# A ViT block in one kernel: other jobs between the last column sums and the output products, turns among the output products, and GpSimd's clearing ahead of its table loads

## Chip, cores, metric

One core of a Trainium2 chip (trn2). The metric is the device time of one execution in microseconds (us); lower is better.

## The reference

Sixty-four images of 224 x 224 x 3 go through patch embedding, one attention layer and a mixture-of-experts feed-forward layer, in float32:

```
h = tok(x)                                # 16x16 patches, layernorm, 768->192, layernorm, cls token, + position
h = concat([cls_tok, h], axis=1)          # (64, 198, 192)
qkv = (layernorm(h) @ qkv_w.T)            # 12 heads of 64
attn = (q @ k.T + q . (tab_kv[iv] + tab_kh[ih])) * scale    # relative positions by row (iv) and column (ih)
attn = softmax(attn)
out = attn @ v + attn . (tab_vv[iv] + tab_vh[ih])
h = h + out.reshape(b, n, 768) @ proj_w.T + proj_b
h = h + shared_mlp(n) + top2_of_8_experts(n)    # n = layernorm(h), hidden relu squared
```

## The kernel before

Three stages follow each other, each with its own buffers and one hand-written program per engine; what one stage computes for the next lies in device memory. `tokens_stage` makes the tokens, `attention_stage` the attention layer, `experts_stage` the rest.

**Tokens stage.** Eight groups of eight images (GROUPS, GB), 14 patch columns (SIDE) each. At a group's end VectorE scales the 14 tiles of normalised rows (L303) and signals `rows_normed`; GpSimd multiplies them by a gain (L221) and adds the positions (L224), and SP's queue stores them. In the last group the work is split: VectorE signals after the first POOLED = 6 tiles, which GpSimd finishes, and finishes the other 8 itself (L311, L315). SP stores the two parts with two DMAs (L156), GpSimd's part first.

**Attention stage, the step.** A group has 16 token tiles and six head pairs (PAIRS); a pair takes 16 steps (8 images x 2 heads), a group 96 steps. Step i of every engine is the same list of pieces. TensorE: scores of step i (L1077), transposes of the probabilities of step i-2 (L1043), the weighted sum of step i-3 (L1060), then the jobs that the table gives to this step. VectorE: the row maximum (L870), the reciprocal of the sums of step i-1 (L862), two copies of the weighted sum of step i-3 (L854, L855), then its part of the jobs. ScalarE: a copy of the transposed probabilities (L712), the exponentials (L724), then its part of the jobs. GpSimd multiplies the probabilities by the reciprocal (L631). Each waits by semaphore for the piece that it reads; the engines run in order, so whoever is behind with a job is behind with the next step.

**Attention stage, the jobs.** `spread` (three times: first, middle and last group) writes the order of the jobs of each pair and spreads them over its 16 steps by COST, a number for each kind. All jobs use four PSUM banks (RING = 4) in turn, in this order, so a job also waits until the job four places ahead of it has been read out. For pair p the jobs are, with the letters of the code:

- f(Q), f(K), f(R), f(C): queries and keys of the next pair (L998), then their products with the row tables (L1002) and column tables (L1008); ScalarE copies the first three kinds, VectorE adds C (L814).
- v: values for two pairs (L1016), copied by ScalarE (L703).
- l(0..3), l(4..7): for the pair just finished, the value-side sums by rows (L1020, added by VectorE at L822) and by columns (L1026, added at L831). l(7) is a short one.
- l(8..15): the output products (L1031), added to the residual by VectorE (L841). l(8) reads all of the column sums, so it waits for l(7)'s addition.
- t(0..7), once per group, for the next group: a turn (L991, L992) transposes two normalised tiles. ScalarE copies the high parts (L681, L682), VectorE writes the low parts (L799, L800) and normalises the two tiles of the turn after next (L780). A query block Q[j] reads turns 2j and 2j+1.

**Attention stage, the opening.** Before the first step the weights are transposed (`prep`, L952 and L953) with the first group's eight turns among them, and the first pair's jobs are done without steps. GpSimd makes the one-hot rows, issues the table DMAs (L612, L613), clears `kx`, `qx` and `rx` (L615, L616, L618), and copies the one-hot rows into `kx` (L624). VectorE spreads the tables (L910, L923) when they have landed; TensorE waits for that, for the copies and for the clearing, and then does `opening[TURN:]`, whose first eight jobs are Q and K.

## Time and profile before

| | |
|---|---|
| median of 3 runs | 4431.72 us (4425.48 to 4433.78) |
| the profiled execution | 4426.74 us, its span 4425.0 us |
| mean granted TensorE clock | 0.963 |
| TensorE busy | 4084.1 us (92%) |
| VectorE busy | 2922.1 us (66%) |
| ScalarE busy | 2506.7 us (57%) |
| GpSimd busy | 1273.7 us (29%) |

The tokens stage lasts until 418 us, the attention stage's opening until 509.6, its steps until about 3488, the experts stage until the end. A busy time counts an instruction from its start to its end, waiting inside it included. The granted clock is a share of 2.4 GHz; it has two levels, 1.00 and 0.50. The page also has an idle time before each group of instructions and what ended it.

### The profile page before, as it was taken

The numbers are of one execution on the slowest core, as the hardware profiler recorded it, in microseconds if no ns is written. First come the engines' busy times: TensorE is split into PE (matmuls) and PEld (weight loads), VectorE is DVE, ScalarE is ACT, GpSimd is POOL, SyncE is SP. The second block draws the span as 40 slices with busy tenths as digits, with TensorE's granted clock in tenths as the row PEclk, the third lists the DMA queues.
The fourth block names the chain that finished last, engine by engine and source line by source line (L and its number), as shares of the span: only waits on it lengthen the run. The fifth ranks groups of instructions, "written<-read, shape, count | busy, mean of one in ns | idle before, by whom it ended". The sixth has DMA issues, their size and how long they took to land. (4 is left out here: it accounts for less than half of the span.)

```text
span 4425.0 us, 84814 instructions
## 1 busy us (share of the span) xinstructions
PE 4084.1 (92%) x28203; PEld 3987.8 (90%) x28203; DVE 2922.1 (66%) x7468; ACT 2506.7 (57%) x6685; POOL 1273.7 (29%) x1423
## 2 busy tenths in 40 slices
PE   4986799899999999989989999999999799999999
PEld 4885699899899999989989998998999699999999
DVE  4675666666666766666666666666666577777776
ACT  2553666566666666656666666666665344444443
POOL 1232322222232222213222222221322244444443
PEclk8997899999999999999999999999999799999999
DMA  8543000000000000000000000000000222222222
GB/s 184 131 109 73 7 1 1 1 24 1 1 23 1 1 2 23 1 1 23 1 1 19 7 1 2 23 1 1 12 1 1 66 90 89 89 89 89 89 89 87
DMA packets 88973, 161.67 MB, mean 37 GB/s; under 512 B 5705, under 2 KB 75936, under 8 KB 85054
## 3 DMA queue, kind: packets, MB, share of 16 engines
q1 hardware_dynamic: 85118, 152.66, 12.1%
q0 software_dynamic: 944, 2.42, 0.3%
q8 instruction: 182, 2.98, 0.3%
q10 hardware_dynamic: 2576, 2.36, 0.2%
q14 instruction: 153, 1.25, 0.1%
HBM read 127.82 MB, written 29.60 MB: 36 GB/s over the span
## 5 line engine op out<-in xcount | busy, mean ns | idle before, releaser
L631 POOL TENSOR_TENSOR att_prob<-att_prob,att_total 99x396 f32<-99x396 f32 x768 | 650.9, 848 | 2279.0 <-DVE att_total L862 2279.0
L712 ACT ACTIVATE att_probT<-att_t 99x396 f32<-99x396 f32 x768 | 385.0, 501 | 737.4 <-PE att_t L1043 732.0
L870 DVE TENSOR_REDUCE att_npeak<-att_s 99x2 f32<-99x396 f32 x768 | 435.4, 567 | 451.7 <-PE att_s L1077 437.2
L724 ACT ACTIVATE att_prob<-att_s,att_npeak 99x198 f32<-99x198 f32 x1536 | 638.0, 425 | 80.3 <-DVE att_npeak L870 77.5
L1077 PE MATMUL att_s<-att_kx,att_qx 96*99 96x198 f32 (+1 forms) x3072 | 661.9, 339 | 4.5 <-DVE att_xres L841 2.3
L1060 PE MATMUL att_o<-att_probT,att_vx 99*96 99x198 f32 (+1 forms) x3072 | 663.1, 339 | 1.1 <-DVE att_rx L855 1.1
L1257 POOL TENSOR_TENSOR ffn_hidden<-ffn_relu 128x384 f32<-128x384 f32 x462 | 419.7, 914 | 494.8 <-ACT ffn_relu L1286 492.7
L1077 PEld LDWEIGHTS att_s<-att_kx,att_qx 96*99 96x99 f32 (+1 forms) x3072 | 494.3, 170 | 16.3 <-issue 5.3
L1286 ACT ACTIVATE ffn_relu<-ffn_h 128x384 f32<-128x384 f32 x462 | 226.3, 490 | 477.3 <-PE ffn_h L1503 476.5
L1515 PE MATMUL ffn_y<-ffn_down,ffn_hidden 128*128 128x192 f32 x2772 | 487.5, 326 | 0.0
L1060 PEld LDWEIGHTS att_o<-att_probT,att_vx 99*96 99x96 f32 (+1 forms) x3072 | 477.2, 181 | 5.8 <-issue 1.4
L1515 PEld LDWEIGHTS ffn_y<-ffn_down,ffn_hidden 128*128 128x128 f32 x2772 | 457.8, 190 | 1.2 <-issue 0.2
L854 DVE COPY att_oT<-att_o 64x198 f32<-64x198 f32 x768 | 277.1, 361 | 240.7 <-PE att_o L1060 233.2
L1043 PEld LDWEIGHTS att_t<-att_ident,att_prob 99*99 99x99 f32 x3072 | 396.1, 170 | 37.5 <-issue 21.9
L1043 PE MATMUL att_t<-att_ident,att_prob 99*99 99x99 f32 x3072 | 405.0, 255 | 20.3 <-ACT att_probT L712 16.5
L855 DVE COPY att_rx<-att_o 32x198 f32<-32x198 f32 x768 | 404.1, 526 | 10.4
L1408 DVE TENSOR_TENSOR ffn_hidden<-ffn_hidden,ffn_gates 64x384 f32<-64x384 f32 (+1 forms) x528 | 362.4, 702 | 20.5 <-issue 3.8
L1031 PE MATMUL att_p<-att_pw,att_oT 128*99 128x192 f32 x1536 | 292.6, 334 | 80.9 <-DVE att_oT L831 80.9
L1031 PEld LDWEIGHTS att_p<-att_pw,att_oT 128*99 128x99 f32 x1536 | 247.7, 169 | 89.6 <-issue 88.1
L724 ACT ACTIVATION_READ_ACCUMULATOR att_prob<-att_s,att_npeak 99x1 f32 x1536 | 313.3, 204 | 0.0
L814 DVE TENSOR_TENSOR att_qx<-att_p,att_qx 32x448 f32<-32x448 f32 (+1 forms) x384 | 226.4, 590 | 63.7 <-PE att_p L1008 35.4
L348 PE MATMUL tok_y<-tok_w,tok_patchT 128*112 128x192 f32 x1344 | 249.6, 339 | 10.5 <-DVE tok_y L282 10.5
(237 smaller groups left out, 8170.7 us busy)
## 6 DMA issues: line engine op xcount, KB each, us to landing
ffn_gates<-gate_rows SPq DMA_DIRECT2D x66, 768.0 KB, 5.0
tok_pixels<-in_x SPq DMA_DIRECT2D x24, 1568.0 KB
ffn_hid<-hidden SPq DMA_DIRECT2D x35, 288.0 KB, 3.0
att_xres<-hidden SPq DMA_DIRECT2D x8, 1188.0 KB
hidden<-att_xres SPq DMA_DIRECT2D x8, 1188.0 KB
ffn_acc<-hidden SPq DMA_DIRECT2D x33, 288.0 KB, 2.9
out_hidden<-ffn_acc SPq DMA_DIRECT2D x33, 288.0 KB, 2.4
hidden<-tok_rows SPq DMA_DIRECT2D x7, 1176.0 KB
```

Source lines behind the costliest of these rows:

```text
L631: nc.gpsimd.tensor_tensor(prob[:, i % 2, :, :], prob[:, i % 2, :, :], view(total[:, i % 2, :], [[1, 2], [0, NTOK]]), ALU.mult).then_inc(pr ...
L712: nc.scalar.activation(probT[:, i % 2, :], t_bank[0:HALF, 0:2 * NTOK], ACT.Copy).then_inc(probT_made, 1)
L724: ins = nc.scalar.activation(prob[:, i % 2, h, :], s_bank[i % 2][0:HALF, h * NTOK:(h + 1) * NTOK], ACT.Exp, bias=npeak[:, i % 2, h:h + 1], ...
L855: nc.vector.tensor_copy(view(rx[ext:ext + 32, p % 2, :], [[GB, NTOK]], b), o_bank[ext:ext + 32, 0:NTOK]).then_inc(outs_used, 1)
L870: nc.vector.tensor_reduce(npeak[:, i % 2, :], s_bank[i % 2][0:HALF, 0:2 * NTOK].rearrange("p (h k) -> p h k", h=2), AX.X, ALU.max, negate= ...
L1031: ins = nc.tensor.matmul(bank[0:HALF, t * DIM:(t + 1) * DIM], oT[:, s, cols], pw[:, weights, :], start=True, stop=True)
L1043: ins = nc.tensor.transpose(t_bank[0:HALF, k * NTOK + h * HALF:k * NTOK + (h + 1) * HALF], prob[:, j % 2, h, k * HALF:(k + 1) * HALF], ide ...
L1060: ins = nc.tensor.matmul(o_bank[0:M, 0:NTOK], vx[:, 2 * b + k, p % 2, v0:v0 + M], probT[:, j % 2, k * NTOK:(k + 1) * NTOK], start=(k == 0) ...
L1077: ins = nc.tensor.matmul(s_bank[i % 2][0:HALF, h * NTOK:(h + 1) * NTOK], qx[0:K, p % 2, head, q0:q0 + HALF], kx[0:K, p % 2, head, b * NTOK ...
L1257: nc.gpsimd.tensor_tensor(hidden[0:rows, s, j, :], relu[0:rows, (n + 2 * s) % 4, :], relu[0:rows, (n + 2 * s) % 4, :], ALU.mult).then_inc( ...
L1408: ins = nc.vector.tensor_tensor(hidden[lo:hi, s, j, :], hidden[lo:hi, s, j, :], gates[lo:hi, s, e, :], ALU.mult)
L1515: ins = nc.tensor.matmul(y_bank[t][:, 0:DIM], hidden[:, s, j, t * 128:(t + 1) * 128], down[:, j, :], start=(n == 0), stop=(n == HT - 1))
```

## The change

1. In the jobs of every pair, l(5) and l(7) go up; l(6, 7), a key or value job and f(C[2], C[3]) stand together ahead of l(8). Before, l(7, 8) were neighbours.
2. Four turns, t(0) to t(3), stand among the output products of the fifth pair of a group (`turning`), one behind each second one. Before, two. The sixth pair (`ending`) begins with the other four.
3. In the opening GpSimd clears `kx` and `qx` right after the one-hot rows, copies into `kx`, clears `rx`, and only then issues the table DMAs. TensorE does the eight Q and K jobs before it waits for tables and buffers.
4. In the last group of the tokens stage POOLED is 5, and GpSimd starts when all 14 tiles are scaled.

```diff
-    POOLED = 6
+    POOLED = 5
...
-                        if wv == (SIDE if more else POOLED) - 1:
-                            ins.then_inc(rows_normed, 1)
+                    ins.then_inc(rows_normed, 1)
                     if not more:
-                        ins.then_inc(last_normed, 1)
-                        dve.wait_ge(last_normed, 1)
+                        dve.wait_ge(rows_normed, GROUPS + PRIMED)
...
                 if ending and not last:
-                    jobs = f(Q[0]) + t(2) + f(K[0]) + t(3) + f(Q[1]) + t(4) + f(K[1]) + t(5) + f(Q[2]) + t(6) + f(K[2])
-                    jobs += t(7) + f(Q[3], K[3]) + l(0) + f(R[0])
+                    jobs = f(Q[0]) + t(4) + f(K[0]) + t(5) + f(Q[1]) + t(6) + f(K[1]) + t(7) + f(Q[2], K[2], Q[3], K[3])
+                    jobs += l(0) + f(R[0])
...
-                jobs += l(4) + f(C[0]) + k(2) + l(5) + f(C[1]) + l(6) + k(3) + f(C[2]) + l(7, 8) + f(C[3])
-                jobs += l(9, 10, 11, 12) + (t(0) if turning else []) + l(13, 14) + (t(1) if turning else []) + l(15)
+                jobs += l(4) + f(C[0]) + l(5) + k(2) + f(C[1]) + l(6, 7) + k(3) + f(C[2], C[3])
+                for j in range(8, 16):
+                    jobs += l(j) + (t((j - 9) // 2) if turning and j % 2 else [])
...
+                nc.gpsimd.memset(kx[:], 0.0).then_inc(keys_cleared, 1)
+                nc.gpsimd.memset(qx[:], 0.0).then_inc(keys_cleared, 1)
+                pool.wait_ge(onehot_made, 9)
+                pool.wait_ge(keys_cleared, 2)
+                for s in range(2):
...
+                pool.wait_ge(keys_made, 4)
+                pool.wait_ge(prep_full, PAIRS)
+                nc.gpsimd.memset(rx[:], 0.0).then_inc(zeroed, 1)
                 for half in range(2):
                     for i, tab in enumerate((tab_kv, tab_kh)):
...
                 spread_onehot()
+                for j in opening[TURN:TURN + 8]:
+                    job(0, -1, "opening", *j)
                 pe.wait_ge(tables_made, 1)
                 pe.wait_ge(keys_made, 4)
                 pe.wait_ge(zeroed, 1)
                 pe.wait_ge(tables_in, 16 * 16)
-                for j in opening[TURN:]:
+                for j in opening[TURN + 8:]:
                     job(0, -1, "opening", *j)
```

TensorE's order in the third pair of the first group, from the third column sum on (L1026 value-side columns, L998 a key block, L1008 query-side columns, L1031 output products; L1077, L1043 and L1060 are the fixed products of a step). Before, the last rows of it:

```order
628 L998 MATMUL att_p<-att_x0h,att_w0h 128x396
...
632 L998 MATMUL att_p<-att_x,att_w1l 128x396
633 L1008 MATMUL att_p<-att_q,att_tq 72x112 x4
634 L1077 MATMUL att_s<-att_kx,att_qx 99x198 x2
635 L1043 MATMUL att_t<-att_ident,att_prob 99x99 x4
636 L1060 MATMUL att_o<-att_probT,att_vx 128x198 x2
637 L1026 MATMUL att_p<-att_rx,att_tv 128x112 x2
638 L1031 MATMUL att_p<-att_pw,att_oT 99x192 x2
```

And now:

```order
627 L1026 MATMUL att_p<-att_rx,att_tv 128x112 x2
628 L998 MATMUL att_p<-att_x0h,att_w0h 128x396
...
632 L998 MATMUL att_p<-att_x,att_w1l 128x396
633 L1077 MATMUL att_s<-att_kx,att_qx 99x198 x2
634 L1043 MATMUL att_t<-att_ident,att_prob 99x99 x4
635 L1060 MATMUL att_o<-att_probT,att_vx 128x198 x2
636 L1008 MATMUL att_p<-att_q,att_tq 72x112 x6
637 L1031 MATMUL att_p<-att_pw,att_oT 99x192 x2
```

The short column product (L1026 x2) has moved ahead of the key block, a step's fixed products and both pieces of query columns (x6); before, the output product was the next row.

TensorE's order at the end of the fifth pair of that group (L991 belongs to a turn, four rows each). Before:

```order
956 L1031 MATMUL att_p<-att_pw,att_oT 99x192 x4
957 L1077 MATMUL att_s<-att_kx,att_qx 99x198 x2
958 L1043 MATMUL att_t<-att_ident,att_prob 99x99 x4
959 L1060 MATMUL att_o<-att_probT,att_vx 96x198 x2
960 L991 MATMUL att_p<-att_ident,att_norm 128x99
...
964 L1031 MATMUL att_p<-att_pw,att_oT 99x192 x2
965 L1077 MATMUL att_s<-att_kx,att_qx 99x198 x2
```

And now:

```order
957 L1031 MATMUL att_p<-att_pw,att_oT 99x192 x2
958 L991 MATMUL att_p<-att_ident,att_norm 128x99
...
962 L1031 MATMUL att_p<-att_pw,att_oT 99x192 x2
963 L1077 MATMUL att_s<-att_kx,att_qx 99x198 x2
964 L1043 MATMUL att_t<-att_ident,att_prob 99x99 x4
965 L1060 MATMUL att_o<-att_probT,att_vx 96x198 x2
966 L1031 MATMUL att_p<-att_pw,att_oT 99x192 x2
967 L991 MATMUL att_p<-att_ident,att_norm 128x99
```

There is a turn in each of the last four steps, where there were turns in two.

GpSimd's order in the opening now (before, the five DMAs stood ahead of the clearing, and the copies last):

```order
48 L608 MEMSET att_kx 128x6336
49 L609 MEMSET att_qx 128x6336
50 L615 COPY att_kx<-att_onehot 32x1584 x4
51 L619 MEMSET att_rx 96x3168
52 L623 DMA att_tabT<-in_L_attn_tab_kv 64x30x1
53 L623 DMA att_tabT<-in_L_attn_tab_kh 64x30x1
54 L623 DMA att_tabT<-in_L_attn_tab_kv 64x30x1
55 L623 DMA att_tabT<-in_L_attn_tab_kh 64x30x1
56 L624 DMA att_pbias<-in_L_attn_proj_b 99x192
```

The clearing has moved up by five DMAs, and the DMAs stand last.

## Rows read from the trace of the kernel before

**Rows 1.** Windows, the steps of the attention stage: length; busy times; clock, DMA share, GB/s.

```profile
core 0: us, PE busy (x) PEld busy (x) DVE busy (x) ACT busy (x) POOL busy (x), PEclk, DMA share, GB/s
509.60:3488.00 2978.40, 2811.90 (x20399) 2752.26 (x20397) 1926.04 (x4671) 1871.08 (x5475) 721.62 (x896) 0.98 0.02 7
```

**Rows 2.** Waits of TensorE, same stretch: us in total, times, longest.

```profile
PE att_p L1031 <- DVE att_oT L831: 80.9, 48, 2.3
PE att_p L998 <- DVE att_x L800: 31.1, 7, 4.4
PE att_p L998 <- issue: 20.2, 14, 2.1
```

**Rows 3.** Timelines of VectorE and TensorE, third pair of the fourth group: start, length.

```profile
1779.42 0.45 DVE L831 TENSOR_TENSOR att_oT<-att_p,att_oT 128x224 f32<-128x224 f32 x1
...
1780.12 0.86 PE L1031 MATMUL att_p<-att_pw,att_oT 128*99 128x192 f32 x4 [1.75 <-DVE att_oT L831]
1780.82 0.83 PE L1077 MATMUL att_s<-att_kx,att_qx 128*99 128x198 f32 x4
...
1782.52 0.55 PE L1008 MATMUL att_p<-att_q,att_tq 128*72 128x112 f32 x4
```

**Rows 4.** Timeline of TensorE, sixth pair of that group.

```profile
1922.82 0.67 PE L998 MATMUL att_p<-att_x0h,att_w0h 128*128 128x396 f32 x1 [4.45 <-DVE att_x L800]
```

**Rows 5.** Windows behind three waits of that group.

```profile
1720.00:1724.00 4.00, 4.00 (x18) 3.58 (x18) 1.20 (x3) 1.22 (x5) 0.85 (x1) 0.57 0.02 4
...
1922.00:1928.00 6.00, 5.18 (x18) 4.91 (x19) 2.02 (x6) 2.88 (x8) 0.85 (x1) 0.50 0.00 0
...
1942.00:1946.00 4.00, 4.00 (x16) 3.82 (x15) 1.07 (x4) 3.60 (x9) 0.85 (x1) 0.57 0.00 0
```

**Rows 6.** Timeline of GpSimd in the opening.

```profile
433.70 1.05 POOL L612 DMA_DIRECT2D att_tabT<-in_L_attn_tab_kv  x1 [9.08 <-issue]
...
436.37 5.40 POOL L615 MEMSET att_kx<- 128x6336 f32 x1
...
449.83 6.18 POOL L624 COPY att_kx<-att_onehot 32x1584 f32<-32x1584 f32 x4
```

**Rows 7.** Timelines of VectorE and TensorE in the opening.

```profile
441.95 7.93 DVE L780 TENSOR_SCALAR att_norm<-att_xres,att_mv,att_sd 99x192 f32<-99x192 f32 x1
...
451.50 0.43 PE L991 MATMUL att_p<-att_ident,att_norm 99*128 99x99 f32 x1 [17.94 <-DVE att_norm L780]
...
454.49 0.35 DVE L799 TENSOR_TENSOR att_x0l<-att_p,att_x0h 128x198 fp32r<-128x198 f32 x1
...
480.85 0.70 PE L998 MATMUL att_p<-att_x0h,att_w0h 128*128 128x396 f32 x1 [2.70 <-DVE att_vx L923]
```

**Rows 8.** The tables' tile: time from issue to landing of its DMAs.

```profile
DMA to landing us min/median/max: 7.4/8.6/9.8
```

**Rows 9.** Timelines of the tokens stage's end; last, the line that waits for the store.

```profile
400.60 8.83 DVE L303 TENSOR_SCALAR tok_rows<-tok_y,tok_mv,tok_rstd 112x192 f32<-112x192 f32 x14
...
402.51 2.68 POOL L221 TENSOR_TENSOR tok_rows<-tok_rows,tok_g 112x1152 f32<-112x1152 f32 x1 [27.79 <-DVE tok_rows L303]
...
411.26 1.76 DVE L315 TENSOR_TENSOR tok_rows<-tok_rows,tok_posb 112x1536 f32<-112x1536 f32 x1
...
L158 SPq EVENT_SEMAPHORE  x1: 17/17/17, 418.2 to 418.2; - x1
```

**Rows 10.** Timelines of GpSimd and VectorE in the experts stage.

```profile
3602.27 0.83 POOL L1257 TENSOR_TENSOR ffn_hidden<-ffn_relu 128x384 f32<-128x384 f32 x1 [2.00 <-ACT ffn_relu L1286]
3602.45 1.05 DVE L1408 TENSOR_TENSOR ffn_hidden<-ffn_hidden,ffn_gates 64x384 f32<-64x384 f32 x1
...
3603.52 0.56 DVE L1408 TENSOR_TENSOR ffn_hidden<-ffn_hidden,ffn_gates 64x384 f32<-64x384 f32 x1
```

**Rows 11.** Windows of a fifth pair's end and the sixth's start; VectorE's timeline at a turn.

```profile
1899.00:1915.00 16.00, 16.00 (x111) 15.56 (x112) 13.41 (x35) 7.09 (x25) 3.39 (x4) 1.00 0.01 2
1915.00:1938.00 23.00, 16.72 (x99) 15.82 (x98) 12.16 (x35) 14.88 (x43) 3.39 (x4) 0.85 0.00 1
...
1907.22 0.36 DVE L799 TENSOR_TENSOR att_x0l<-att_p,att_x0h 128x198 fp32r<-128x198 f32 x1 [0.28 <-ACT att_x L682]
...
1907.99 0.67 DVE L780 TENSOR_SCALAR att_norm<-att_xres,att_mv,att_sd 99x192 f32<-99x192 f32 x2
```

More of the change, by code:

```diff
@@ L114, in tokens_stage @@
         channel_in = [m.sem(f"channel_in{c}") for c in range(CH)]
-        last_normed, last_scaled, last_made = m.sem("last_normed"), m.sem("last_scaled"), m.sem("last_made")
+        last_scaled, last_made = m.sem("last_scaled"), m.sem("last_made")
         consts_in, weights_in, ident_made = m.sem("consts_in"), m.sem("weights_in"), m.sem("ident_made")
@@ L607, in _ @@
                 nc.gpsimd.tensor_tensor(onehot[:, :], onehot[:, :], rowhot, ALU.add).then_inc(onehot_made, 1)
+                nc.gpsimd.memset(kx[:], 0.0).then_inc(keys_cleared, 1)
[3 more added lines that the diff above has]
+                for s in range(2):
+                    for lo, head in ((64, 0), (32, 1)):
+                        pool.wait_ge(keys_made, 2 * s + head)
+                        nc.gpsimd.tensor_copy(view(kx[lo:lo + 32, s, head, :], [[NTOK, GB], [1, NTOK]]),
+                                              view(onehot[:, :], [[0, GB], [1, NTOK]])).then_inc(keys_made, 1)
+                pool.wait_ge(keys_made, 4)
+                pool.wait_ge(prep_full, PAIRS)
+                nc.gpsimd.memset(rx[:], 0.0).then_inc(zeroed, 1)
                 for half in range(2):
@@ L614, in _ @@
                                ).then_inc(consts_in, 16)
-                nc.gpsimd.memset(kx[:], 0.0).then_inc(keys_cleared, 1)
-                nc.gpsimd.memset(qx[:], 0.0)
-                pool.wait_ge(prep_full, PAIRS)
-                nc.gpsimd.memset(rx[:], 0.0).then_inc(zeroed, 1)
-                pool.wait_ge(zeroed, 1)
-                pool.wait_ge(keys_cleared, 1)
-                for s in range(2):
-                    for lo, head in ((64, 0), (32, 1)):
-                        pool.wait_ge(keys_made, 2 * s + head)
-                        nc.gpsimd.tensor_copy(view(kx[lo:lo + 32, s, head, :], [[NTOK, GB], [1, NTOK]]),
-                                              view(onehot[:, :], [[0, GB], [1, NTOK]])).then_inc(keys_made, 1)
                 pool.wait_ge(consts_in, 16 * 5)
```

## The prediction

> **What bounds the kernel now.** The page's shares (in the table above) say that TensorE is the busiest engine by far, so time can only go where TensorE stands still or runs at its lower clock. The windows say how much of that the attention stage holds [rows 1]: 2978.4 us with TensorE busy 2811.9, so 166 us idle, and a mean granted clock of 0.98. The waits of TensorE in that stage name the idle time [rows 2]: 80.9 us in 48 waits of an output product (L1031) for a sum of VectorE (L831), 31.1 us in 7 waits of a query product (L998) for a turned tile (L800), and 20.2 us in 14 more at L998, which the profile calls "issue". The timelines then show each kind once.
>
> First kind [rows 3]: VectorE does the short last sum at 1779.42 to 1779.87, and the first output product, which reads it, starts at 1780.12 after 1.75 us of idle time. In the order it is the job right behind the product that this sum is made of.
>
> Second kind [rows 4]: a query product starts at 1922.82 after 4.45 us. It needs turn 3, and turn 3 is the job right ahead of it in the order; ScalarE's copies of a query and a key block stand in that queue ahead of the turn's. Turns 5 and 7 have the same neighbours, which are the 14 waits of 1.4 us.
>
> The clock [rows 5]: it is granted at 0.57 in the 4 us that begin with the end of such an L1031 wait, which is 1.7 us lost; two of these in this group of images make 3.4 us. Behind the 4.45 us wait it is 0.50 for 6 us (1.2 GHz, 3.0 us lost), and at 1942 it falls again (0.57, 1.7 us): with the 0.3 us until it is back, 5.0 us per group.
>
> **The opening, in steps.** GpSimd has two table DMAs issued by 424.6, then 9.08 us pass, and its clearing only begins at 436.37; the copies of the one-hot rows end it [rows 6]. VectorE's first normalise starts at 441.95 and takes 7.93 us where two of them take 0.67 elsewhere [rows 7, 11]: it ends when the third clearing ends, at 449.8. The next three end with one GpSimd copy each, so the first low part starts at 454.49. In the change the two large clearings stand at 422.5 to 433.3, the four copies to 439.5, the third clearing to 442.2. The normalises then meet 0.2 us of it. TensorE's first turn (451.50 now) comes at about 442.7, and the low part 1.6 us behind it, when ScalarE has copied, at 444.3. From there VectorE is busy without a gap, so all of it shifts: **-10.2 us** (bounds -13 and -5: clearing gone wholly, or DMA issues in the way as a copy is now, about 1.5 us for each normalise).
>
> The table DMAs move behind that: issued from 442.2, with the same 14 us of issuing, and 7.4 to 9.8 us to land [rows 8], they are there at about 465. VectorE wants them when preparation ends, 477.5 - 10.2 = 467.3. If they were 7 us late nobody on the path would mind, for the eight query and key products now go ahead of the wait for tables. TensorE's first stands at 480.85 behind 2.70 us of idle time, released by the last table copy [rows 7]: **-2.7** (bounds -3.2, -1). ScalarE takes 11 us for these eight, and that covers the tables; its own wait, for the key buffers, is met far earlier.
>
> **The last group of the tokens stage.** Now the 14 scalings take 8.83 us, since two of them stand behind GpSimd's operations of 2.68 us, then VectorE's own two take 1.76 each and end at 413.02 [rows 9]. In the change all 14 run undisturbed (0.29 us apart, ending at 404.7), but then two-input operations of both engines start together: VectorE with 9 tiles (1.98 us each), GpSimd with 5 (2.2 each). Such a pair stands in the experts stage [rows 10]: VectorE's product, started 0.18 us behind GpSimd's, takes 1.05 us against 0.56, so it waits for it. In turns they end at 404.8 + 8.3 = 413.1, GpSimd probably last; and SP's queue issues the 5-tile store first, so both stores start there. The last landing is now 5.2 us behind VectorE's end [rows 9], with 8 tiles on the way; with 14 it is between 0 and 3.9 us more (6 x 5.2 / 8), and I take **+2.5 us**. Unhindered, both would end at 409.3 and it would be -1.5. The Trainium skill ("SBUF — State Buffer", Who interferes with whom) has a rule against this edit: a VectorE operation with two SBUF inputs and a GpSimd operation that reads SBUF exclude each other for their whole length. The trace agrees (1.05 against 0.56 us), so the sum goes by +2.5 and not by -1.5.
>
> **Between last column sums and output products.** The short product now goes up; behind it come a key or value product, the fixed products of a step (1.7 us, from 1780.82 to 1782.52 [rows 3]), and the last two pieces of query columns, then the first output product: about 3.8 us of TensorE work, in which VectorE has some 2 us of its own ahead of the sum. Of 80.9 us, 2.0 stay (the last pair of the last group and the closing have nothing to put between), 16.1 (7 x 2.3, the longest, in the pair with turns) belong to the next term, and of the remaining 62.8 I keep 3: **-60 us** (bounds -63, -45). What is late next is the pile on VectorE behind it: both pieces of query columns and a residual sum in one step, by my count 4.2 us against TensorE's 3.5. The probabilities of two steps on are then ready 0.2 us before they are wanted; the -45 is for that cover gone.
>
> **Turns among output products.** Four turns instead of two fall in the last steps of the fifth pair. There VectorE is already busy 13.41 of 16 us while TensorE is 16.00 of 16 [rows 11]. Each turn costs it 1.35 us (two low parts and two normalises, 1907.22 to 1908.57), two more make 16.1, and it waits up to half a microsecond for ScalarE at each. So VectorE becomes the limit. In the sixth pair there are then four turns instead of six, the first two queries need turns long done, and the last two have another product between. Following the new order by hand with these durations I get six waits of 0.4 to 1.6 us, 5.6 in all per group, against (16.1 + 31.1 + 20.2) / 7 = 9.6 now: 7 x 4.0 = **-28 us** (bounds 0 and -67).
>
> **Clock.** The 3.4 us per group around plain waits is 27 us in 8 groups; with the waits goes most of it, **-24** (bounds -27, 0). Of 5.0 us in each of 7 groups I expect 2.1 to stay, since waits of 1.6 us can bring it: **-20** (bounds -35, 0).
>
> **Sum:** -10.2 - 2.7 + 2.5 - 60 - 28 - 24 - 20 = -142.4. The profiled execution took 4426.7 us; the median of the three runs, 4431.7, is 0.1% above. 4426.7 - 142.4 = 4284. The experts stage is not touched.
>
> **Rivals.** *The turn stretch stays as it is* (4332 us): VectorE's pile brings as much waiting as before, and the clock falls as often; -94.4 only. For it speaks 13.41 of 16; against it that no single wait can be as long as the 4.45. *Nothing is left* (4224 us): all 67 us and all 62 us of clock come back and the opening gives its 13: +2.5 - 13 - 63 - 67 - 62 = -202.5. *The waits move* (4400 us): L1031's wait turns into one of the transposes (L1043) for GpSimd's product, whose slack is 0.2 us by my count; the opening's 10.4 and some 15 us stay. *Slower* (4526 us): between the middle of the fifth pair and that of the sixth the many short waits hold TensorE at 1.2 GHz throughout. The stretch holds 16.0 + 16.7 = 32.7 us of its work [rows 11], which costs 7 x (32.7 - 5.0) = +194 against -94.4. It decides from the point where the clock is low for 57% of that work (7 x 32.7 x 0.57 - 35 = 95). Against it: over 23 us with 6.3 us idle, the 4.45 us in one piece, the mean clock was still 0.85 [rows 11]. The Trainium skill ("TensorE: Matmul & The Clock Gate", A second HAM failure mode: psum-queue depth-cycling) describes this mechanism: frequent short idle times between groups of products make the gate swing between its levels. The trace has single falls, no such series.
>
> **Chances.** Forecast 0.58 (4255 to 4315), turn stretch unchanged 0.20, nothing left 0.08, waits move 0.09, slower 0.05. The range 4235 to 4345 takes the first two and a little of the third. 0.2%, 9 us, is about what a measurement of this kernel can tell from no change: faster 0.93, same 0.02, slower 0.05.
>
> **What would show it.** L780's longest falls from 7.93 to under 3 us; the first L998 comes 10 to 13 us earlier (some 470); L1031 waits for L831 only once or twice; L998 has no 4 us wait; the stage's clock is 0.99; waits of 0.4 to 1.6 us appear at L1043 and L1060 around the fifth and sixth pair. I am wrong if L1043's waits exceed 60 us, or if the clock stays at 0.98.

## The result and the profile after

The changed kernel takes 4251.28 us (median of 4 runs, 4251.08 to 4252.45), the kernel before 4432.75 us (4 runs, 4425.48 to 4436.11): ratio 0.9595, 95% interval 0.9581 to 0.961. The forecast was 4284 us in a range of 4235 to 4345, so the measured time lies in the range, 33 us below the forecast and 27 us above the nearest rival (4224). The gain is 181 us where 142 were forecast.

Its page, with the lines that stand in the table of before:

```profile
span 4249.3 us, 84755 instructions
PE 4023.5 (95%) x28203; PEld 3931.1 (93%) x28203; DVE 2890.2 (68%) x7468; ACT 2501.6 (59%) x6685; POOL 1274.0 (30%) x1423
PEclk8998799999999999999999999999999899999999
```

The span divides at two events: the first score product (L1077) and the first transpose of the experts stage (L1472).

| us | before | after | difference |
|---|---|---|---|
| up to the first scores | 509.8 | 496.0 | -13.7 |
| steps of the attention stage | 2987.1 | 2825.1 | -162.0 |
| experts stage | 928.1 | 928.1 | 0 |

**The steps.** Windows over them in both kernels (length, TensorE busy, clock), of after:

```profile
core 0: us, PE busy (x) PEld busy (x) DVE busy (x) ACT busy (x) POOL busy (x), PEclk, DMA share, GB/s
495.90:3306.20 2810.30, 2752.98 (x20399) 2695.74 (x20397) 1905.62 (x4670) 1866.53 (x5475) 720.47 (x896) 1.00 0.02 7
```

Of before, the same stretch was 2972.20 us with 2811.80 busy. So TensorE stood idle for 160.4 us and now for 57.3: 103.1 us less. The other 58.8 us are the same 20,399 products done faster, which is the clock. Read in windows of 2 us, with (1 - granted clock) added up, the steps lost 71.7 us in 34 falls of the clock, and now lose 10.3 us in 2, one at 540 and one at the very end of the stage. The turn stretch of the fourth group, of which [rows 11] have the windows, stands some 85 us earlier now (both kernels are in the last steps of the fifth pair in the first window, and in the first of the sixth in the second):

```profile
1814.00:1830.00 16.00, 14.32 (x102) 13.31 (x100) 14.48 (x39) 7.14 (x26) 3.04 (x4) 1.00 0.01 2
1830.00:1853.00 23.00, 20.46 (x136) 18.95 (x135) 17.36 (x48) 18.75 (x59) 5.42 (x7) 1.00 0.00 1
```

VectorE is busy 14.48 of 16 us, more than TensorE's 14.32: it is the fuller engine there, as the prediction feared. But the 23 us behind it hold 20.46 us of TensorE at full clock, where they held 16.72 at 0.85.

The waits of TensorE in the steps (us in total, times, longest), against [rows 2]:

```profile
PE att_t L1043 <- POOL att_prob L631: 29.7, 37, 1.3
PE att_t L1043 <- ACT att_probT L712: 16.2, 18, 1.3
PE att_p L1031 <- DVE att_oT L831: 2.0, 2, 1.2
```

L1031's 48 waits (80.9 us) are 2 (2.0 us), and both kinds at L998 (51.3 us) are gone. New are the waits at L1043 for GpSimd's scaled tile, 3.9 us before. 78.9 + 51.3 - 25.8 = 104.4 is close to the 103.1 of the windows. The wait for ScalarE was 16.5 us before and is not the change's.

The new waits stand where turns lie among output products. VectorE's and GpSimd's rows ahead of such a wait in the third group, and TensorE's rows with a wait there (start, length):

```profile
1470.76 1.02 DVE L841 TENSOR_TENSOR att_xres<-att_p,att_xres 99x384 f32<-99x384 f32 x2
1471.69 0.56 DVE L870 TENSOR_REDUCE att_npeak<-att_s 99x2 f32<-99x396 f32 x1
1472.16 0.16 DVE L862 RECIPROCAL att_total<-att_total 99x2 f32<-99x2 f32 x1
1472.40 0.85 POOL L631 TENSOR_TENSOR att_prob<-att_prob,att_total 99x396 f32<-99x396 f32 x1 [3.43 <-DVE att_total L862]
```

```profile
1473.30 0.59 PE L1043 MATMUL att_t<-att_ident,att_prob 99*99 99x99 f32 x4 [1.30 <-POOL att_prob L631]
1477.11 0.59 PE L1043 MATMUL att_t<-att_ident,att_prob 99*99 99x99 f32 x4 [0.20 <-POOL att_prob L631]
1480.98 0.59 PE L1043 MATMUL att_t<-att_ident,att_prob 99*99 99x99 f32 x4 [0.94 <-POOL att_prob L631]
1489.40 0.59 PE L1043 MATMUL att_t<-att_ident,att_prob 99*99 99x99 f32 x4 [1.33 <-POOL att_prob L631]
```

GpSimd is free, but gets its reciprocal late, since VectorE has a turn's writes, two residual sums (L841) and a maximum ahead of it: the pile that the prediction saw, five waits and 4 us a group. No fall of the clock stands behind any of these waits.

**The opening.** The four first normalises in one row, before:

```profile
441.95 12.62 DVE L780 TENSOR_SCALAR att_norm<-att_xres,att_mv,att_sd 99x192 f32<-99x192 f32 x4
```

VectorE's and GpSimd's timelines of after, against [rows 6, 7]:

```profile
432.62 4.26 DVE L758 BATCH_NORM_STATS2 att_stat<-att_xres 99x6 f32<-99x192 f32 x16 [7.96 <-DMA att_xres<-hidden]
439.98 3.29 DVE L780 TENSOR_SCALAR att_norm<-att_xres,att_mv,att_sd 99x192 f32<-99x192 f32 x4
443.82 0.36 DVE L799 TENSOR_TENSOR att_x0l<-att_p,att_x0h 128x198 fp32r<-128x198 f32 x1 [0.56 <-ACT att_x L682]
```

```profile
422.04 5.37 POOL L608 MEMSET att_kx<- 128x6336 f32 x1
427.36 5.37 POOL L609 MEMSET att_qx<- 128x6336 f32 x1
432.86 6.17 POOL L615 COPY att_kx<-att_onehot 32x1584 f32<-32x1584 f32 x4
439.10 2.73 POOL L619 MEMSET att_rx<- 96x3168 f32 x1
447.05 1.05 POOL L623 DMA_DIRECT2D att_tabT<-in_L_attn_tab_kv x1 [3.08 <-issue]
```

The four normalises took 12.6 us in all, each ending at about the end of a GpSimd operation; now they take 3.29. The first low part comes at 443.82 rather than 454.49. The gap before the third table transfer is 3.08 us where it was 9.08 [rows 6], and the tables' tile lands faster than in [rows 8]:

```profile
DMA to landing us min/median/max: 3.6/3.8/4.2
```

TensorE's first query product, against the 480.85 of [rows 7], comes at once behind the last work before it:

```profile
466.72 0.51 PE L965 MATMUL att_s<-att_ident,att_onehot 32*99 32x32 f32 x2 [4.17 <-DVE att_w1l L773]
467.15 0.70 PE L998 MATMUL att_p<-att_x0h,att_w0h 128*128 128x396 f32 x1
```

**The last group of tokens**, VectorE and GpSimd, against [rows 9]:

```profile
399.00 4.15 DVE L303 TENSOR_SCALAR tok_rows<-tok_y,tok_mv,tok_rstd 112x192 f32<-112x192 f32 x14
403.18 1.96 DVE L309 TENSOR_TENSOR tok_rows<-tok_rows,tok_g 112x1728 f32<-112x1728 f32 x1
405.18 3.84 DVE L313 TENSOR_TENSOR tok_rows<-tok_rows,tok_posb 112x1728 f32<-112x1728 f32 x1
...
403.23 3.98 POOL L221 TENSOR_TENSOR tok_rows<-tok_rows,tok_g 112x960 f32<-112x960 f32 x1 [30.04 <-DVE tok_rows L303]
407.28 3.80 POOL L224 TENSOR_TENSOR tok_rows<-tok_rows,tok_posb 112x960 f32<-112x960 f32 x1
```

They end in turns, some 2 us apart: VectorE's at 405.14, GpSimd's at 407.21, VectorE's at 409.02, GpSimd's at 411.08.

The tokens stage ahead of L298 scatters by up to 4 us from one profile to another, so the opening is compared in two pieces that don't: from L298 to the wait that ends the tokens stage (L158), and from there to the first scores. The first is 17.9 us before and 19.1 in the nine profiles with the new token group; the second is 91.6 before, 78.2 after, and 78.1 to 78.3 in all seven experiments that leave the opening as changed.

### The profile page after: what moved, and what is told of

Its sections match the earlier page's. It is cut to its first block and busy times, and to the rows that moved or that the text cites. A ratio compares the mean times of both kernels' runs of the same rounds, so it can differ in the third digit from the quotient of the medians.

```text
span 4249.3 us, 84755 instructions
## 1 busy us (share of the span) xinstructions
PE 4023.5 (95%) x28203; PEld 3931.1 (93%) x28203; DVE 2890.2 (68%) x7468; ACT 2501.6 (59%) x6685; POOL 1274.0 (30%) x1423
## 3 DMA queue, kind: packets, MB, share of 16 engines
q1 hardware_dynamic: 85118, 152.66, 12.6%
q14 instruction: 153, 1.25, 0.1%
## 5 line engine op out<-in xcount | busy, mean ns | idle before, releaser
L712 ACT ACTIVATE att_probT<-att_t 99x396 f32<-99x396 f32 x768 | 384.8, 501 | 570.5 <-PE att_t L1043 565.0
L1060 PE MATMUL att_o<-att_probT,att_vx 99*96 99x198 f32 (+1 forms) x3072 | 652.4, 334 | 1.1 <-DVE att_rx L855 1.1
L1077 PE MATMUL att_s<-att_kx,att_qx 96*99 96x198 f32 (+1 forms) x3072 | 642.2, 331 | 4.8 <-DVE att_xres L841 2.6
L1077 PEld LDWEIGHTS att_s<-att_kx,att_qx 96*99 96x99 f32 (+1 forms) x3072 | 480.1, 165 | 12.8 <-issue 5.6
L1060 PEld LDWEIGHTS att_o<-att_probT,att_vx 99*96 99x96 f32 (+1 forms) x3072 | 468.3, 178 | 4.9 <-issue 1.4
L1043 PEld LDWEIGHTS att_t<-att_ident,att_prob 99*99 99x99 f32 x3072 | 380.9, 166 | 79.7 <-POOL att_prob L631 54.8
L1043 PE MATMUL att_t<-att_ident,att_prob 99*99 99x99 f32 x3072 | 401.4, 253 | 47.3 <-POOL att_prob L631 29.7
L855 DVE COPY att_rx<-att_o 32x198 f32<-32x198 f32 x768 | 404.1, 526 | 10.4
L1031 PE MATMUL att_p<-att_pw,att_oT 128*99 128x192 f32 x1536 | 283.9, 327 | 2.0 <-DVE att_oT L831 2.0
L346 PE MATMUL tok_y<-tok_w,tok_patchT 128*112 128x192 f32 x1344 | 248.0, 337 | 10.3 <-DVE tok_y L282 10.3
L1031 PEld LDWEIGHTS att_p<-att_pw,att_oT 128*99 128x99 f32 x1536 | 247.0, 166 | 3.6 <-issue 2.4
```

The source lines that it names most:

```text
L712: nc.scalar.activation(probT[:, i % 2, :], t_bank[0:HALF, 0:2 * NTOK], ACT.Copy).then_inc(probT_made, 1)
L855: nc.vector.tensor_copy(view(rx[ext:ext + 32, p % 2, :], [[GB, NTOK]], b), o_bank[ext:ext + 32, 0:NTOK]).then_inc(outs_used, 1)
L1031: ins = nc.tensor.matmul(bank[0:HALF, t * DIM:(t + 1) * DIM], oT[:, s, cols], pw[:, weights, :], start=True, stop=True)
L1043: ins = nc.tensor.transpose(t_bank[0:HALF, k * NTOK + h * HALF:k * NTOK + (h + 1) * HALF], prob[:, j % 2, h, k * HALF:(k + 1) * HALF], ide ...
L1060: ins = nc.tensor.matmul(o_bank[0:M, 0:NTOK], vx[:, 2 * b + k, p % 2, v0:v0 + M], probT[:, j % 2, k * NTOK:(k + 1) * NTOK], start=(k == 0) ...
L1077: ins = nc.tensor.matmul(s_bank[i % 2][0:HALF, h * NTOK:(h + 1) * NTOK], qx[0:K, p % 2, head, q0:q0 + HALF], kx[0:K, p % 2, head, b * NTOK ...
```

## Experiments

The time to compare with is the changed kernel's 4251.28 us; "steps" are those of the table above. The experiments ran in three later series, in which the kernel before had medians of 4430.65 to 4432.68 us (4432.75 beside the changed kernel). Times of two series that lie only 2 or 3 us apart therefore show little by themselves, and such differences are read from stretches of the profiles.

**One: the table transfers ahead of the clearing again.**

```diff
+                for half in range(2):
+                    for i, tab in enumerate((tab_kv, tab_kh)):
...
+                pool.dma_start(pbias[:, :], bass.AP(tensor=proj_b.tensor, offset=proj_b.offset, ap=[[0, HALF], [1, DIM]])
...
                 nc.gpsimd.memset(kx[:], 0.0).then_inc(keys_cleared, 1)
                 nc.gpsimd.memset(qx[:], 0.0).then_inc(keys_cleared, 1)
...
                 nc.gpsimd.memset(rx[:], 0.0).then_inc(zeroed, 1)
-                for half in range(2):
-                    for i, tab in enumerate((tab_kv, tab_kh)):
...
```

> The changed kernel with one thing undone: GpSimd issues its table DMAs ahead of the clearing again (the new order of clearing, copies, clearing stays). Theory 1 (VectorE's normalises stand behind GpSimd's writes): the clearing of qx and the four copies then meet the normalises, the four L780 take about 11 us instead of 3.3, the first scores come 8 to 11 us later (504 to 507 us instead of 495.9), total about 4260 us. Rival (what the opening gained came from other things, such as the load of the residual landing earlier): L780 stays short and the first scores come within 3 us of 495.9. If the scattered table DMAs also hold up the load of the residual, it lands 2 us later (statistics start at 434.6 instead of 432.6).

4259.87 us (4257.74 to 4261.63), +8.6; from L158 to the first scores 85.4 us, +7.2. VectorE:

```profile
435.37 4.26 DVE L758 BATCH_NORM_STATS2 att_stat<-att_xres 99x6 f32<-99x192 f32 x16 [10.28 <-DMA att_xres<-hidden]
442.74 7.05 DVE L780 TENSOR_SCALAR att_norm<-att_xres,att_mv,att_sd 99x192 f32<-99x192 f32 x4
```

The order of transfers and clearing is worth 7 to 9 us, and the normalises beside GpSimd's clearing and copies are stretched again, though to 7.05 us and not to the 11 expected. The first row shows a second part: the load of the residual is used 17.2 us behind L158, against 14.8. The prediction has no term for it.

**Two: tables ahead of the first query and key products.**

```diff
-                for j in opening[TURN:TURN + 8]:
-                    job(0, -1, "opening", *j)
                 pe.wait_ge(tables_made, 1)
...
-                for j in opening[TURN + 8:]:
+                for j in opening[TURN:]:
```

> The changed kernel with TensorE waiting for tables and buffers ahead of its first eight query and key products, as before. Theory: 2.7 us of idle time come back between the one-hot transposes and the first query product, first scores at 498.6 us instead of 495.9, total +2.7 us (about 4254). Rival (ScalarE paces that part anyway, or the clock eats it): first scores within 1 us of 495.9.

4255.05 us (4253.79 to 4256.05), and 80.9 us from L158 to the first scores, +2.7; the wait of before is back, with its length:

```profile
470.40 0.70 PE L998 MATMUL att_p<-att_x0h,att_w0h 128*128 128x396 f32 x1 [2.70 <-DVE att_vx L923]
```

Of the 13.4 us that this stretch lost, one and two give 7.2 + 2.7. If the two simply add, the other 3.5 lie in what neither undoes, the copies ahead of the third clearing: before, that clearing (2.7 us) stood ahead of the copies and moved them back. That is argued from the rows; neither it nor one and two together was tried.

**Three: the old place of the last column sums, the new turns.**

```diff
-                jobs += l(4) + f(C[0]) + l(5) + k(2) + f(C[1]) + l(6, 7) + k(3) + f(C[2], C[3])
-                for j in range(8, 16):
+                jobs += l(4) + f(C[0]) + k(2) + l(5) + f(C[1]) + l(6) + k(3) + f(C[2]) + l(7, 8) + f(C[3])
+                for j in range(9, 16):
```

> The changed kernel with the old order of the last column sums (7 and 8 neighbours again), turns as in the change. Theory (the waits L1031 for L831 are what this edit removed, and with each of them now and then a fall of the clock): 48 waits come back, 75 to 95 us of idle time, and some 25 us of lower clock: steps of the attention stage 100 to 115 us longer, total about 4360 us. Rival (the sums edit gives little, the wait would only move to the transposes L1043): under 40 us longer, total under 4295. Rival for the clock (falls belong to the turns alone): the stage's busy time of TensorE stays at 2753 us within 5.

**Four: the old turns, the new place of the sums.**

```diff
-                    jobs = f(Q[0]) + t(4) + f(K[0]) + t(5) + f(Q[1]) + t(6) + f(K[1]) + t(7) + f(Q[2], K[2], Q[3], K[3])
-                    jobs += l(0) + f(R[0])
+                    jobs = f(Q[0]) + t(2) + f(K[0]) + t(3) + f(Q[1]) + t(4) + f(K[1]) + t(5) + f(Q[2]) + t(6) + f(K[2])
+                    jobs += t(7) + f(Q[3], K[3]) + l(0) + f(R[0])
...
-                for j in range(8, 16):
-                    jobs += l(j) + (t((j - 9) // 2) if turning and j % 2 else [])
+                jobs += l(8, 9, 10, 11, 12) + (t(0) if turning else []) + l(13, 14) + (t(1) if turning else []) + l(15)
```

> The changed kernel with the old places of the turns (two among output products, six in the sixth pair), sums as in the change. Theory: the waits at L998 come back, 7 x 7.3 = 51 us, the L1043 waits for GpSimd fall from 29.7 to under 8 us, and the clock falls in the sixth pair, 7 x 5 = 35 us: net 65 to 80 us longer, total about 4325 us. Rival (the turns' edit was worth what I predicted, 28 + 20 us): 48 us longer, total 4299. Rival (the waits at L998 were only long because TensorE had stood at L1031 before): under 25 us longer.

**Nine: both orders as in the kernel before,** with the new opening and token group.

> The kernel before with only the change's opening (the clearing on GpSimd first, tables behind Q and K, the token groups): both job orders as before. Theory (the two job edits explain all of the steps' gain and the opening is additive): the steps take 2987 us again, the opening keeps its 13.8 us, and the time is 4432.7 - 14 = 4419 us, 4414 to 4424. Rival (part of the steps' 162 us came from the opening's edits, a start at another phase): the steps take less than 2975 us and the time is below 4408.

| kernel | time, us | steps, us | TensorE idle, us | clock lost, us (falls) |
|---|---|---|---|---|
| changed | 4251.28 | 2825.1 | 57.3 | 10.3 (2) |
| three, sums old | 4327.51 (4325.81 to 4329.54) | 2900.2 | 108.5 | 29.0 (13) |
| four, turns old | 4294.24 (4293.31 to 4298.31) | 2871.9 | 78.9 | 44.4 (16) |
| nine, both old | 4412.9 (4410.37 to 4424.31) | 2985.4 | 155.2 | 78.5 (35) |

The waits of TensorE in the steps, of three:

```profile
PE att_p L1031 <- DVE att_oT L831: 54.4, 34, 1.8
PE att_t L1043 <- POOL att_prob L631: 27.4, 30, 1.3
```

of four (the kernel is a line shorter there, so L998 is L997 and L1043 is L1042):

```profile
PE att_p L997 <- DVE att_x L799: 31.0, 7, 4.4
PE att_p L997 <- issue: 17.6, 14, 2.0
PE att_t L1042 <- POOL att_prob L630: 2.3, 4, 0.8
PE att_p L1030 <- DVE att_oT L830: 2.0, 2, 1.2
```

and of nine:

```profile
PE att_p L1030 <- DVE att_oT L830: 80.9, 48, 2.3
PE att_p L997 <- DVE att_x L799: 31.1, 7, 4.5
```

Nine confirms that the steps' gain is that of the two orders, to within 2 us (2985.4 against 2987.1), and that the opening adds to it; its median came 1 us under the span of times expected.

Three is 76 us slower, where about 109 were expected, and lies between theory and rival; TensorE's busy time rose from 2753.0 to 2776.8 us, so falls of the clock belong to these waits too. Four is 43 us slower, where the theory had 65 to 80: it is the rival, the turns' worth as predicted (48), that came out. The waits and the lost clock came back as the theory said (48.6 us at L998, 34.1 us of clock), but the waits at L1043 went away for it (2.3 us are left), and part of the low clock lies in idle time, where it costs nothing: the steps grew by 46.8 us, 21.6 of it idle and 25.2 busy.

From nine to four, the sums alone are worth 113.5 us; from four to the changed kernel, the turns are worth another 46.8. In the other order it is 85.2 for the turns and 75.1 for the sums. Three says why it is not the same: 34 waits at L1031 are left and not 48, because `spread` deals a pair's jobs out over its 16 steps by their share of the cost. With other numbers of turns in the fifth and sixth pairs, l(7) and l(8) fall into neighbouring steps there, and a step's fixed products come to lie between the short sum and the first output product. TensorE's order in the fifth pair of three (here with the buffers' numbers):

```order
968 L1026 MATMUL att_p2<-att_rx,att_tv 128x112 x2
969 L1077 MATMUL att_s1<-att_kx,att_qx 99x198 x2
970 L1043 MATMUL att_t<-att_ident,att_prob 99x99 x4
971 L1060 MATMUL att_o<-att_probT,att_vx 96x198 x2
972 L1031 MATMUL att_p3<-att_pw,att_oT 99x192 x2
```

So 14 waits (80.9 - 54.4 = 26.5 us) go with either edit. They are most of the 38.4 us by which the two edits' worths from the side of the changed kernel (75.1 + 46.8 = 121.9) fall short of the 160.3 that nine has over it; the rest is in the clock (18.7 + 34.1 us lost against 68.2).

**Five: statistics and normalisations 8 steps earlier.**

```diff
-    STATS, DEVIATION = 40, 72
+    STATS, DEVIATION = 32, 64
```

> The changed kernel, with the statistics and deviations of a group due at steps 32 and 64 rather than 40 and 72, so that the turns and normalisations start some 8 steps earlier. Theory (the waits that are left, TensorE's at L1043 for the turn's GpSimd copy, 29.7 us in 37, come from the pile of turns and scaled tiles in the last steps of a group): they fall below 15 us and the time is 4251 less 10 to 20, 4231 to 4241 us. Rival (a turn waits on its own copies however early it stands): the waits stay at 25 to 35 us and the time within 5 us of 4251.

4265.77 us (4264.13 to 4266.85), 14.5 slower, which neither expected. The waits for GpSimd fell only to 22.1 us in 30: the table of jobs holds the turns where they were (the expectation had them move too), and only the normalising is earlier. The waits for ScalarE rose from 16.2 (18 times) to 27.2 (25 times), one of 1.6 us in each of 7 groups, and the clock lost 22.2 us in 6 falls, where the changed kernel lost 10.3 in 2. The steps are 17.1 us longer, 5.4 of it idle time; three of the falls stand right behind one of the seven waits of 1.6 us. ScalarE's timeline in such a place, with TensorE's wait:

```profile
1072.81 1.28 ACT L670 ACT_TABLE_LOAD   x1
1074.11 0.31 ACT L670 ACTIVATE att_sd<-att_mv,att_eps 99x16 f32<-99x16 f32 x1
1074.32 0.48 ACT L712 ACTIVATE att_probT<-att_t 99x396 f32<-99x396 f32 x1
1074.82 1.28 ACT L724 ACT_TABLE_LOAD   x1
...
1078.74 0.88 ACT L686 ACTIVATE att_q<-att_p 128x396 f32<-128x396 f32 x1
```

```profile
1081.13 0.56 PE L1043 MATMUL att_t<-att_ident,att_prob 99*99 99x99 f32 x4 [1.62 <-ACT att_probT L712]
```

The square root brings two table loads, 2.6 us of ScalarE, and 8 steps earlier they fall just ahead of the copies of query blocks, and the copy for which TensorE waits (L712) comes late. With 72 no wait of the kind is longer than 1.3 us.

**Six: the tables' transfers and the bias on ScalarE's queue,** behind its weight loads; GpSimd issues none.

> The changed kernel, with the opening's table and bias transfers issued by ScalarE behind its weight loads, none by GpSimd. Theory (GpSimd's scattered table transfers share the queues' engines with the first load of the residual and hold its landing up): VectorE's first statistics start 1 to 2 us earlier than 432.6 us if the table transfers are behind that load, and the wait of 7.96 us ahead of them is shorter. Rival (the load of the residual is set by the stores and tokens before it): the statistics start at 432.6 within 0.3 us. In both the total stays within 4 us of 4251, since ScalarE pays for the issues.

4259.43 us (4258.11 to 4265.06), outside of what both expected: the five issues keep ScalarE from 420.98 to 444.8 us and so hold back its splitting of the weights, on which VectorE then waits.

```profile
448.12 0.29 DVE L771 TENSOR_TENSOR att_w0l<-att_t,att_w0h 128x128 fp32r<-128x128 f32 x1 [9.73 <-ACT att_w1h L664]
450.03 1.25 DVE L780 TENSOR_SCALAR att_norm<-att_xres,att_mv,att_sd 99x192 f32<-99x192 f32 x4
```

The statistics start at 432.81 (15.2 us behind L158, 14.8 in the changed kernel), as the rival had it. The tables were not behind the load, as the theory wanted, but were issued beside it, from 420.98 on; issued there by ScalarE they did not move its use to the 16.4 and 17.2 us that it has with GpSimd's issues ahead of it. The second row gives a price that could not be had before: with the clearing over, the four normalises take 1.25 us, so in the changed kernel 2.0 us of stretching are still there.

**Seven: the last token group on VectorE alone,** in two halves of seven tiles with a store behind each; GpSimd has none of it.

> The changed kernel, with the last group of token tiles wholly on VectorE (two halves of seven tiles, a store behind each), GpSimd idle there. Theory (VectorE and GpSimd shut each other out, so that the four parts, 1.96 + 3.98 + 3.84 us behind the table step, run one after the other): the stretch from the one-hot step to the load's first use gets 2 to 4 us shorter and the total is 4247 to 4249. Rival (GpSimd's parts lie beside VectorE's, and VectorE alone is longer): the stretch gets 1 to 4 us longer, 4252 to 4255.

4248.42 us (4246.84 to 4249.79), as the theory had it; the intervals of the two ratios to the kernel before overlap, and it is the stretch that shows the gain: from L298 to L158 it is 15.4 us instead of 19.1. Four operations of 1.56 us follow each other, of which the first two are:

```profile
405.29 1.56 DVE L310 TENSOR_TENSOR tok_rows<-tok_rows,tok_g 112x1344 f32<-112x1344 f32 x1
406.88 1.56 DVE L313 TENSOR_TENSOR tok_rows<-tok_rows,tok_posb 112x1344 f32<-112x1344 f32 x1
```

From the first of them to the last one's end it is 6.2 us; the two engines in turns took 7.9 (403.18 to 411.08). The other 2 us lie between the last operation's end and L158 (4.7 us where it was 6.7); that they come from the first half's store, which leaves half-way, is argued and was not tried by itself. The Trainium skill ("SBUF — State Buffer", Who interferes with whom) has the two engines exclude each other for operations of this kind; by that rule the shared group takes the sum of all four durations. The trace agrees: the four ends in turns, each some 2 us behind the one before it, make the 7.9.

**Ten: the reciprocal first.**

```diff
+                        if v != "first" or i >= 1:
+                            inverted_sums(n, i)
                         dve.wait_ge(scores, n + 1)
                         nc.vector.tensor_reduce(npeak[:, i % 2, :], ...
-                        if v != "first" or i >= 1:
-                            inverted_sums(n, i)
```

> The changed kernel, with VectorE's reciprocal of the step before's sums (L862) ahead of the maximum over this step's scores (L870), in every step. Theory (the wait at L1043 in the turning steps is GpSimd's scaled tile, late because the 0.16 us reciprocal stands behind the 0.56 us maximum, which waits for the scores, on a VectorE full of turn copies): the L1043 waits for GpSimd, 29.7 us in 37, fall to 10 to 20 us and the time is 4234 to 4245 us. Rival (what comes first is only traded: the maximum and so the exponentials are 0.16 us later in each step, and TensorE waits for ScalarE's copies instead): the waits for ScalarE, 16.2 us, grow by as much as the others shrink, and the time is 4248 us or more.

4249.83 us (4248.92 to 4251.44). The waits for GpSimd fell by 4.7 us only, those for ScalarE did not grow, and the steps are 1.1 us shorter:

```profile
PE att_t L1043 <- POOL att_prob L631: 25.0, 37, 1.2
PE att_t L1043 <- ACT att_probT L712: 16.0, 17, 1.3
```

Two neighbouring rows of VectorE, where a turn stands among output products:

```profile
1474.04 0.55 DVE L841 TENSOR_TENSOR att_xres<-att_p,att_xres 99x384 f32<-99x384 f32 x1
1474.51 0.15 DVE L862 RECIPROCAL att_total<-att_total 99x2 f32<-99x2 f32 x1
```

The theory did not hold; of the rival the time did (4248 us or more), but not its reason. TensorE's idle time in the steps fell by 4.7 us, but its busy time rose by 3.5. In VectorE's queue the reciprocal still stands behind the residual's sums (L841, 0.55 us each) and the next normalise (0.67), which says that the pile makes it late more than the maximum ahead of it; no run takes the pile away.

**Eleven: seven and ten together.**

> The kernel with that reciprocal first and with the last token group on VectorE alone. Theory (the two lie in different stages and add): its time is that of the reciprocal kernel less 2 to 4 us. Rival (the token edit's 2.9 us was the scatter between runs): the two kernels take the same time within 1 us.

4245.83 us (4245.09 to 4247.96), 4.0 less than ten on the same chip, as the theory had it (2 to 4). This is the fastest version; its ratio to the kernel before is 0.9589, 0.9576 to 0.9602, and beside the changed kernel's own interval that does not set them apart. Within one series, its five runs all lie under all five of ten.

## Why the prediction was right, and where its sizes were off

The mechanisms were in the main as forecast, and the time lies in the range. But the sums, the clock and the opening all gave more than forecast, and so 4251 us lies just outside the 4255 to 4315 that the forecast itself was given, between it and the rival *nothing is left*.

**The opening: forecast -10.4, measured -13.7.** From L158 to the first scores it was -13.4 against -10.2 - 2.7 = -12.9. The table step was right to the tenth (experiment two). In the clearing's -10.2 two things were missed that nearly cancel: the load of the residual is used 1.6 us sooner (what the table transfers do to it stood in no term), and so the normalises begin at 439.98 and not 441.95. That puts the first of them back into the third clearing (1.96 us for it), and the third takes 0.83 us beside GpSimd's first table issue: 2.0 us of stretch in all where 0.2 was counted. **The token group** cost +1.2 us (17.9 to 19.1) and not +2.5: the four operations alternated as said and ended 12.4 us behind L298 (12.8 by the forecast), and the last landing followed 6.7 us later, where 7.6 was counted. The rest of the -13.7 is the tokens stage ahead of it, 1.6 us earlier in this profile, which is scatter.

**Last sums: forecast -60.** L1031's waits went from 80.9 to 2.0 with this edit and without the turns' (experiment four), so it is -78.9, outside the bounds of -63 and -45. The step that failed is the division: "16.1 (7 x 2.3, the longest, in the pair with turns) belong to the next term". Either edit takes these away, and the 7 of 1.5 us in the sixth pair with them. The mechanism, 3.8 us of TensorE work between the sum and its reader, was right, and its cover was never gone.

**Turns: forecast -28.** By that term's own sum, 5.6 us of waits in each of 7 groups instead of 9.6: all of the 9.6 went, and 25.8 / 7 = 3.7 came, so the size of what is kept was off. With the 16.1 counted to the sums, 51.3 - 25.8 = 25.5 us are left for the turns, and experiment four shows them as 78.9 - 57.3 = 21.6 us of idle time. The form was nearly as followed: five waits a group of 0.2 to 1.3 us and not six of 0.4 to 1.6, behind a full VectorE; they are all at L1043, none at L1060 for this reason.

**Clock: forecast -44, measured -58.8.** The step that failed is "of 5.0 us in each of 7 groups I expect 2.1 to stay, since waits of 1.6 us can bring it". None stayed, and 7 x 2.1 = 14.7 us is the difference of 14.8. That this fits to the tenth is chance: by the windows of 2 us the clock gave back 61.4, so the 3 us that the prediction let stay around plain waits went as well. The longest of the new waits are 1.3 us, the work between two of them is some 3 to 7 us, and the clock stood at 1.00 through all of them.

**The rivals.** *Turn stretch unchanged* falls with experiment four: restoring the old turns costs 43 us. *Waits move to L1043* was half right as a place; its size is 25.8 us more, and all waits at L1043 make 45.9 us, below the 60 named. *Slower by the low clock in the stretch* needed the clock low for 57% of it; it was low for none. The Trainium skill ("TensorE: Matmul & The Clock Gate", A second HAM failure mode: psum-queue depth-cycling) describes a kernel in which frequent short idle times make the clock swing. Here five waits of up to 1.3 us within 25 us, in each of seven groups, did not, so the trace does not show it. *Nothing is left* (4224) came nearer than the forecast, 27 us off against 33: the clock gave back nearly all, and the opening its 13, as that rival says; only the idle time did not all go, 25.8 us of it having come up at L1043.

In all, the profiled executions differ by 4425.0 - 4249.3 = 175.7 us where the terms sum to 142.4: 3.3 more in the opening, 15.1 in idle time, 14.8 in the clock. The medians differ by 6 us more, since the profiled execution of before was one of its quicker ones (4426.7).

## To carry to other kernels

A product that reads what the product before it is turned into waits for the other engine's whole answer; one or two independent jobs between them take the wait away, and where waits bring the clock down, this pays again (58.8 us of clock for 103.1 us of idle time). When two edits can remove the same wait, count it once, say that either takes it, and try each edit with and without the other, since worths from one side alone don't add up (75.1 + 46.8 against 160.3). Before a step is shared out over two engines, look for a row in which the two run side by side: here one engine alone took 6.2 us for what the two took 7.9 for.

## What was not expected of the hardware

- With the table transfers of a few KB issued by GpSimd ahead of SyncE's large load of the residual, that load is used later: 16.4 and 17.2 us behind L158 with the tables first (before and experiment one), 14.5 to 15.2 us in the other ten profiles. Among these ten is experiment six, where the same transfers were issued beside the load by ScalarE (15.2 us). Issued behind it by GpSimd, the tables landed in 3.8 us and not 8.6, and the gap in issuing them was 3.1 us and not 9.1. What in the queues does this was not tried.
- The clock's falls went with the length of waits, and how close they lie, more than with their number: 55 waits at L1043, the longest 1.3 us, left 2 falls in the steps; with the same number there, seven of them of 1.6 us (experiment five), there were 6. Three of these came right behind one of the seven, among them the wait of 1.62 us shown, and one behind a wait of 1.5 us at L1077; so such a wait can bring a fall, and in four of the seven places did not. Nor is the length of one wait all: in the kernel before, the clock falls at 1942.3 [rows 5] behind two waits close together, 0.78 us until 1939.49 and 0.97 us until 1941.73, and at the same place of three later groups. The five waits of the changed kernel have 3 to 7 us of work between them.
- The four normalises take 12.6 us beside GpSimd's clearing and copies, 3.29 us beside part of them, 1.25 us beside nothing.
